# Transposing the context's fp16 halves by a DMA instead of on TensorE, in a four-stage kernel on one core

## The chip, the cores and the metric

The kernel runs on one core of one Trainium2 chip, in one launch. The metric is the device time of a run in microseconds. Three runs of the kernel before gave 470.05, 475.46 and 472.96 us, a median of 472.96 us. The profile is of one further execution, which took 474.49 us.

## The reference, cut to what matters

```python
# x: (32, 128, 256), ctx_1024: (32, 128, 256), all fp32
x = x + tanh(g_xattn[0]) * scan(layernorm(x), ctx, ctx)     # running sum of ctx * ctx with decay 0.9, times layernorm(x)
x = x + tanh(g_ffn[0])   * adapters(layernorm(x))           # x @ W.T, plus one of four low-rank adapters, picked per row
x = x + tanh(g_xattn[1]) * attention(layernorm(x), ctx, mask, Wq, Wk, Wv, Wo)
#       head_k = ctx @ Wk,  head_v = ctx @ Wv,  head_q = layernorm(x) @ Wq,  16 heads of 16,
#       sigmoid scores instead of a softmax, masked, then @ Wo
x = x + tanh(g_ffn[1])   * experts(layernorm(x))            # the best two of eight experts for each token
```

The change touches only how `ctx` gets in front of the two products `ctx @ Wk` and `ctx @ Wv`.

## The kernel before, in words

**Tiling.** The 32 batches go through in 16 pairs. One pair is 2 x 128 tokens of 256 features, and it passes stages named after their layer norms: A (the running sum), B (base and adapter product), C (queries and attention), E (router). Pairs overlap: while attention of pair p is under way, the key product of pair p + 2 is made. After the pairs, 39 tiles of 256 routed rows go through two expert layers, and the outputs are gathered and added. Each engine has its whole program written out in a fixed order (`block.sync`, `block.gpsimd`, `block.scalar`, `block.tensor`, `block.vector`); engines meet only at semaphores, and an engine that waits holds back all that stands behind it.

**Split precision.** A large product is made in three fp16 products: the high halves, and high times low both ways (`split_mm`, L1643 to L1652). So each operand exists as a high part (fp32 rounded to fp16) and a low part (fp32 minus high part, rounded).

**The context.** TensorE contracts over partitions, so it needs features on partitions, while `ctx` arrives with tokens on partitions. Before the change, for every pair p:
- SyncE loads `c_in[p % 2]` (`load_ctx`, L466).
- TensorE transposes four 128 x 128 fp32 blocks into the PSUM bank T (`transpose_ctx`, L1704, through `transposes`, L1659). The bank is shared with the transposes of B, C and E, and each waits until the one before it in the order has been copied out.
- ScalarE copies the bank to fp16 `ct_hi` (`hi_ctx`, L1075, through `hi`, L1019). VectorE subtracts and writes `ct_lo` (`lo("T", ...)`, L2456).
- TensorE makes the keys (`keys`, L1725) straight behind it, and about 10 us later the values (`values`, L1735).

ScalarE also squares `c_in` for the running sum (`squared`, L1034).

**SyncE's queue.** SyncE issues the loads, and the trip by which keys and queries are laid out by head: `keep_parts` (L476) writes a 256 KB piece to DRAM, `stack_keys` (L486, 4 DMAs) and `stack_queries` (L499, 8 DMAs) read it back to other partitions. `scores` (L1751) of a pair wait for both stacks. The queue is in order: an issue whose semaphore is not there holds all that follow.

Of the kernel before, what the change touches and what calls it, by code (L numbers as in the profile page):

```python
# [28 lines left out]
F16 = mybir.dt.float16  # L29
# [7 lines left out]
KT = D // 128  # L37
# [8 lines left out]
PROBS = 2  # L46
TOP = 2
# [36 lines left out]
def build(nc, x, ctx, mask, gates_in, temp, bp, sim, wall, wp, wu, wo, w_in, b_in, w_out, b_out, decay, eye, before,  # L84
          routing, y_rows_in, left_rows_in, out):
    st = ExitStack()
    with st:
# [140 lines left out]
        ct_hi = right("ct_hi", [128, KT, 256], F16)  # L228
        ct_lo = right("ct_lo", [128, KT, 256], F16)
# [227 lines left out]
        def _(sp):  # L457
# [158 lines left out]
            load_ctx(5)  # L616
            stack_queries(1)
# [13 lines left out]
            zero_first(7)  # L631
            stack_queries(2)
# [5 lines left out]
            stack_queries(3)  # L638
            stack_keys(4)
# [4 lines left out]
            keep_parts("q", 4)  # L644
            stack_queries(4)
# [6 lines left out]
            stack_queries(5)  # L652
            keep_parts("k", 6)
# [5 lines left out]
            stack_queries(6)  # L659
            keep_parts("k", 7)  # L660
# [6 lines left out]
            keep_parts("k", 8)  # L667
            stack_queries(7)
# [5 lines left out]
            stack_queries(8)  # L674
            keep_parts("k", 9)
# [4 lines left out]
            keep_parts("k", 10)  # L680
            stack_queries(9)
# [10 lines left out]
            stack_queries(10)  # L692
            load_ctx(14)
# [7 lines left out]
            stack_queries(11)  # L701
            keep_parts("k", 12)
# [3 lines left out]
            stack_keys(12)  # L706
            stack_queries(12)
            keep_parts("q", 13)
            stack_keys(13)
            stack_queries(13)  # L710
# [13 lines left out]
            for i in range(2, TILES):  # L724
                load_block(i)

            for n in range(NP):
                load_outputs(n)
                if PICK_BUFS - 1 <= n < ON_SP - 1 + PICK_BUFS:
                    store_pair(n + 1 - PICK_BUFS)  # L730
            for i in range(PICK_BUFS):
                sp.wait_ge(s_out[i], 16 * len(range(i, NP, PICK_BUFS)) + (16 if i == (NP - 1) % PICK_BUFS else 0))
# [3 lines left out]
        def _(pool):  # L736
# [37 lines left out]
            paused = itertools.count(2)  # L774

# [212 lines left out]
            for i in range(4, TILES):  # L988
                keep_block(i, 0)
                if i < CLOSE:  # L990
                    long_pause()
                keep_block(i, 1)

        @block.scalar
        def _(act):
# [244 lines left out]
            sigmoids(0, 1, 1)  # L1240
            sigmoids(0, 1, 0)
# [6 lines left out]
            hi_ctx(3)  # L1248
# [15 lines left out]
            normed_e(0)  # L1264
            sigmoids(1, 2, 0)
# [8 lines left out]
            hi_ctx(4)  # L1274
# [12 lines left out]
            sigmoids(2, 2, 1)  # L1287
            normed_e(1)
# [10 lines left out]
            hi_ctx(5)  # L1299
# [11 lines left out]
            normed_e(2)  # L1311
            sigmoids(3, 2, 1)
# [10 lines left out]
            hi_ctx(6)  # L1323
# [16 lines left out]
            normed_e(3)  # L1340
            gate_sigmoids(6)
# [7 lines left out]
            hi_ctx(7)  # L1349
# [14 lines left out]
            sigmoids(5, 2, 0)  # L1364
            sigmoids(5, 3, 1)
# [8 lines left out]
            hi_ctx(8)  # L1374
# [13 lines left out]
            part_hi("q", 7)  # L1388
            normed_e(5)
# [8 lines left out]
            hi_ctx(9)  # L1398
# [11 lines left out]
            sigmoids(7, 1, 0)  # L1410
            sigmoids(7, 2, 1)
# [11 lines left out]
            hi_ctx(10)  # L1423
# [11 lines left out]
            normed_e(7)  # L1435
            sigmoids(8, 2, 1)
# [10 lines left out]
            hi_ctx(11)  # L1447
# [14 lines left out]
            output_rows(7)  # L1462
            gate_sigmoids(11)
# [8 lines left out]
            hi_ctx(12)  # L1472
# [16 lines left out]
            normed_e(9)  # L1489
            sigmoids(10, 2, 0)  # L1490
# [9 lines left out]
            hi_ctx(13)  # L1500
# [10 lines left out]
            normed_e(10)  # L1511
            sigmoids(11, 2, 1)
# [8 lines left out]
            hi_ctx(14)  # L1521
# [11 lines left out]
            sigmoids(12, 1, 0)  # L1533
            sigmoids(12, 2, 1)
# [9 lines left out]
            hi_ctx(15)  # L1544
# [82 lines left out]
            for i in range(9, TILES + 1):  # L1627
                if i < TILES:
                    copy_hi(i)
                gelu(i - 1)  # L1630
                hidden_hi(i - 1)
            keep_pair(ON_SP)
            for n in range(TAIL, NP):
                copy_x3(n)
            for n in range(ON_SP + 1, NP - 1):
                keep_pair(n)
            for b in range(2):
                keep_batch(NP - 1, b)
# [3 lines left out]
        def _(pe):  # L1642
# [81 lines left out]

            def keys(last, p):  # L1725
# [9 lines left out]
            def values(last, p):  # L1735
                pe.wait_ge(s_lo["T"], p + 1)
                bank_j_free(last, "v")
                for b in range(2):
                    ins = split_mm(bank_j[:, b, :], halves(ct_hi, ct_lo, b), [wcols(k, C_V, D) for k in range(KT)])
                ins.then_inc(s_part["v"], 1)  # L1740
# [196 lines left out]
            transpose_ctx(("B", 2), 3)  # L1937
# [12 lines left out]
            transpose_c(("T", 3), 2)  # L1950
# [23 lines left out]
            transpose_ctx(("E", 0), 4)  # L1974
            project(1)
            keys(("v", 3), 4)
            transpose_c(("T", 4), 3)
# [387 lines left out]
            for i in range(7, TILES + 2):  # L2365
                if i < TILES:
                    transpose_block(i)
# [1680 lines left out]
```

## Time and profile before

| | |
|---|---|
| median of three runs | 472.96 us (470.05 to 475.46) |
| profiled execution, its time | 474.49 us |
| its span | 472.6 us |
| TensorE clock granted, mean of the span | 0.969 |
| busy: PE / DVE / ACT / POOL | 394.9 / 368.8 / 331.4 / 268.7 us |

The span is the time from the first to the last instruction that the profile shows. Busy time of an engine is the sum of its instructions' time. Matmuls are pipelined: the duration of one is longer than the distance to the next, so for TensorE the distance between starts tells what an instruction costs. "Idle before, releaser" is idle time of an engine ahead of an instruction and what ended it. Time "issue" is time in which an engine waited for nothing that the profile shows; a DMA that lands can hide in it.

### The profile page before, as it was taken

What the parts mean: (1) busy time and instruction counts of PE and PEld (TensorE: products, weight loads), DVE (VectorE), ACT (ScalarE), POOL (GpSimd) and SP (SyncE); (2) the same over time, 40 slices, a digit from 0 to 9 for tenths busy, and PEclk for the clock granted to TensorE, in tenths of its full rate; (3) what the DMA queues carried; (4) which work ended last, traced back from release to release, by engine and by line L of the source; (5) the groups of instructions that cost most, each with busy time, mean ns of one, the idle gap of its engine ahead of it and who ended that gap; (6) DMA issues with size and microseconds to landing.
All of it is one profiled execution on the core that took longest, in us unless ns stands there. A gap on an engine that the chain in (4) does not pass through costs nothing.

```text
span 472.6 us, 13099 instructions
## 1 busy us (share of the span) xinstructions
PE 394.9 (84%) x4092; PEld 308.3 (65%) x4092; DVE 368.8 (78%) x1416; ACT 331.4 (70%) x671; POOL 268.7 (57%) x313
## 2 busy tenths in 40 slices
PE   2758899998999989999899987789559999979850
PEld 1536667776776777677686765568438897967740
DVE  2888888998988889899789786367655667779994
ACT  2855788898889889898879877566706666646640
POOL 2522112545454364626545565769988888888870
PEclk9998999999999999999999999899959999999996
DMA  7245576664565555875553774624335569396985
GB/s 242 83 139 163 180 214 179 196 181 141 177 213 170 166 171 167 221 204 184 180 174 111 223 220 121 198 68 130 101 126 143 170 175 332 116 341 251 323 275 204
DMA packets 69500, 87.10 MB, mean 184 GB/s; under 512 B 9485, under 2 KB 55290, under 8 KB 69306
## 3 DMA queue, kind: packets, MB, share of 16 engines
q1 hardware_dynamic: 60074, 65.81, 46.7%
q0 software_dynamic: 6816, 18.65, 10.8%
q10 hardware_dynamic: 2544, 1.81, 1.2%
q8 instruction: 35, 0.57, 0.5%
q14 instruction: 31, 0.25, 0.2%
HBM read 51.07 MB, written 35.18 MB: 182 GB/s over the span
## 4 chain that ended last, share of the span: by engine, by line
PE 42%; POOL 17%; issue 14%; DVE 10%; DMA 8%; ACT 6%; ACTq 0%; POOLq 0%; DVEq 0%; SPq 0%
PE ps_J L1650 12%; PE ps_F L1650 6%; POOL store_y L771 6%; DMA store_y<-y_out,y_row 6%; PE ps_O L1764 5%; PE ps_T L1659 5%; POOL store_x L765 5%; PE ps_S L1751 5%; POOL pause_t L778 5%; PE ps_R L1689 2%; PE ps_O L1775 2%; PE ps_G L1650 2%; DMA temp_t<-in_temp 1%; DVE y_out L2934 1%; DVE xb_lo L2903 1%
## 5 line engine op out<-in xcount | busy, mean ns | idle before, releaser
L771 POOL DMA_INDIRECT store_y<-y_out,y_row x78 | 81.4, 1044 | 21.8 <-issue 16.5
L765 POOL DMA_INDIRECT store_x<-xn_E,slot_u x64 | 68.0, 1063 | 26.5 <-DVE slot_u L2633 13.6
L1089 ACT ACTIVATE prob<-ps_S 128x512 f32<-128x512 f32 x128 | 72.4, 594 | 12.7 <-PE ps_S L1751 10.0
L778 POOL TENSOR_TENSOR pause_t<-half_ones,minus_half 128x2 f32<-128x2 f32 x71 | 54.7, 770 | 1.9
L1751 PE MATMUL ps_S<-q_stack,k_stack 128*128 128x256 f16 x256 | 44.5, 276 | 5.9 <-issue 3.8
L2922 DVE TENSOR_TENSOR h_lo<-h_f,h_hi 128x512 f16<-128x512 f32 x39 | 26.9, 689 | 21.0 <-ACT h_hi L1173 9.4
L1650 PE MATMUL ps_J<-wout_hi,h_hi 128*128 x112 | 31.2, 278 | 14.3 <-DVE y_out L2934 10.9
L1764 PE MATMUL ps_O<-prob,v_wide 128*32 128x128 f32 x1024 | 41.0, 279 | 1.1 <-ACT prob L1089 0.5
L1165 ACT ACTIVATE h_f<-ps_F,bin_t 128x256 f32<-128x256 f32 x56 | 23.4, 470 | 24.5 <-PE ps_F L1650 18.9
L751 POOL TENSOR_TENSOR rstd_C<-var_C,minus_half 128x2 f32<-128x2 f32 x16 | 12.1, 759 | 40.4 <-DVE var_C L2412 40.4
L1650 PE MATMUL ps_F<-xb_hi,win_hi 128*128 128x256 f16 x112 | 31.7, 283 | 3.9 <-DVE xb_lo L2903 3.3
L1751 PEld LDWEIGHTS ps_S<-q_stack,k_stack 128*128 128x128 f16 x256 | 21.7, 98 | 17.3 <-issue 10.4
L1775 PE MATMUL ps_O<-wo_t,av 128*128 128x256 f32 x128 | 31.2, 387 | 1.9 <-ACT av L1117 1.5
L1764 PEld LDWEIGHTS ps_O<-prob,v_wide 128*32 128x32 f32 x1024 | 24.2, 109 | 12.3 <-issue 10.2
L1650 PE MATMUL ps_F<-xb_lo,win_hi 128*128 128x256 f16 x112 | 31.6, 283 | 0.0
L1650 PE MATMUL ps_F<-xb_hi,win_lo 128*128 128x256 f16 x112 | 31.5, 281 | 0.0
L1650 PE MATMUL ps_J<-wout_hi,h_lo 128*128 x112 | 31.1, 278 | 0.0
L1650 PE MATMUL ps_J<-wout_lo,h_hi 128*128 x112 | 31.1, 278 | 0.0
L1152 ACT ACTIVATE xb_hi<-ps_R 128x512 f16<-128x512 f32 x28 | 16.6, 594 | 19.6 <-PE ps_R L1826 15.9
L751 POOL TENSOR_TENSOR rstd_E<-var_E,minus_half 128x2 f32<-128x2 f32 x16 | 11.8, 737 | 31.0 <-DVE var_E L2412 30.8
L756 POOL TENSOR_TENSOR inv_norm<-norm2c,minus_half 128x2 f32<-128x2 f32 x16 | 11.1, 694 | 32.2 <-DVE norm2c L2481 32.2
L1775 PEld LDWEIGHTS ps_O<-wo_t,av 128*128 128x128 f32 x128 | 23.1, 190 | 6.8 <-ACT av L1117 3.5
(301 smaller groups left out, 1399.5 us busy)
## 6 DMA issues: line engine op xcount, KB each, us to landing
parts_scratch<-parts SPq DMA_DIRECT2D x32, 256.0 KB
k_stack<-parts_scratch SPq DMA_DIRECT2D x64, 128.0 KB
q_stack<-parts_scratch SPq DMA_DIRECT2D x128, 64.0 KB
xb<-store_x SPq DMA_DIRECT2D x30, 257.0 KB
y_got<-store_y SPq DMA_DIRECT2D x14, 512.0 KB
c_in<-in_ctx SPq DMA_DIRECT2D x16, 256.0 KB
x_in<-in_x SPq DMA_DIRECT2D x16, 256.0 KB
store_x<-zeros SPq DMA_DIRECT2D x15, 257.0 KB, 4.6
```

The costliest lines, as they stand in the source:

```text
L751: pool.tensor_tensor(rstd[k][q][:, :], var[k][q][:, :], minus_half[:, 0:2], ALU.pow)\
L765: pool.indirect_dma_start(store_x, bass.IndirectOffsetOnAxis(slot_u[q][:, at:at + 1], 0), xn_e[q][:, at, :], None).then_inc(s_scat[q], 16)
L771: pool.indirect_dma_start(store_y, bass.IndirectOffsetOnAxis(y_row[n][:, b:b + 1], 0), y_out[n][:, b, :], None).then_inc(s_y_kept[n], 16)
L778: pool.tensor_tensor(pause_t[:, :], half_ones[:, :], minus_half[:, 0:2], ALU.pow).then_inc(s_set_p, 1)
L1089: act.activation(prob[m % PROBS][:, 2 * n:2 * n + 2, :, :], bank_s[n], ACT.Sigmoid, scale=float(HD) ** -0.5).then_inc(s_prob[n], 1)
L1165: act.activation(h_f32[q][:, m, :], hid_banks[side(i)][:, m, :], ACT.Gelu_apprx_tanh, bias=biases[:, bass.ds(at + m, 1)]).then_inc(s_gelu, 1)
L1650: ins = pe.matmul(o, l, r, start=start and i == 0, stop=stop and i == len(seq) - 1, skip_group_check=skip)
L1659: ins = pe.transpose(bank_t[:, i, b, :], src[:, b, 128 * i:128 * i + 128], ident[:, :])
L1751: ins = pe.matmul(bank_s[n][:, g % 2, :, :], k_stack[q][:, g, k, cut], q_stack[q][:, :, g, k, cut], start=True, stop=True)
L1764: ins = pe.matmul(bank_av[32 * g:32 * g + 32, k, b, :], v_wide[q][:, b, 4 * k + g, 2 * h:2 * h + 2, :].rearrange("p a d -> p (a d)"), prob ...
L1775: ins = pe.matmul(bank_o[:, b, :], av[:, k, b, :], wo_t[:, k, :], start=(k == 0), stop=(k == KT - 1))
L2922: dve.tensor_tensor(h_lo[q][:, :, :], h_f32[q][:, :, :], h_hi[q][:, :, :], ALU.subtract) .then_inc(s_h_lo, 1)
```

## The change

For pairs 0 to 2 all is as before (`PE_CTX = 3`). From pair 3 on, the split into high and low part is made on the tokens-on-partitions layout, straight from `c_in` in SBUF into one piece `c_parts` (128 x 1024 fp16: for each of the parts, each feature half and each batch, one 128 x 128 block). One DMA, issued by SyncE, transposes the eight blocks from SBUF into `ct[p % 2]`, also in SBUF. `c_parts` and the second `ct` lie in room of the fp32 weights (`w_f32`), which is no longer needed by then. The four TensorE transposes of these pairs are gone. `keys` and `values` wait for the DMA's semaphore (`s_decay`, used again) instead of for the low part.

```diff
+PE_CTX = 3
...
-        ct_hi = right("ct_hi", [128, KT, 256], F16)
-        ct_lo = right("ct_lo", [128, KT, 256], F16)
+        ct = [right("ct", [128, 2 * KT, 256], F16),
+              w_f32[:, 0, C_K:C_Q].bitcast(F16).rearrange("p (x c) -> p x c", x=2 * KT)]
+        c_parts = w_f32[:, 1, C_K:C_Q].bitcast(F16).rearrange("p (x c) -> p x c", x=2 * KT * 2)
...
             def load_ctx(p):
-                need(sp, s_t["T"], p - 1)
+                need(sp, s_lo["T"], p - 1)
...
+            def turn_ctx(p):
+                sp.wait_ge(s_lo["T"], p + 1)
+                sp.wait_ge(s_part["k"], p - 1)
+                sp.wait_ge(s_part["v"], p - 1)
+                sp.dma_start(ct[p % 2].rearrange("p x (b s) -> p (x b) s", b=2), c_parts.rearrange("p x c -> p (x c)"),
+                             transpose=True).then_inc(s_decay, 16)
...
             def hi_ctx(p):
-                need(act, s_part["k"], p)
-                need(act, s_part["v"], p)
-                hi("T", p, ct_hi[:, :, :])
+                if p < PE_CTX:
+                    need(act, s_part["k"], p)
+                    need(act, s_part["v"], p)
+                    hi("T", p, ct[0][:, 0:KT, :])
+                    return
+                if p == PE_CTX:
+                    act.wait_ge(s_wlo, 4)
+                act.wait_ge(s_c[p % 2], 16 * (p // 2 + 1))
+                act.wait_ge(s_decay, turned(p - 1))
+                act.activation(c_parts[:, 0:2 * KT, :].rearrange("p (k b) c -> p k b c", b=2),
+                               c_in[p % 2][:, :, :].rearrange("p b (k c) -> p k b c", k=KT), ACT.Copy).then_inc(s_hi["T"], 1)
...
+            def ctx_turned(p):
+                if p < PE_CTX:
+                    pe.wait_ge(s_lo["T"], p + 1)
+                else:
+                    pe.wait_ge(s_decay, turned(p))
...
             def keys(last, p):
-                pe.wait_ge(s_lo["T"], p + 1)
+                ctx_turned(p)
                 bank_j_free(last, "k")
-                feature_major("k", C_K, ct_hi, ct_lo)
+                feature_major("k", C_K, *ctx_parts(p))
...
+            def lo_ctx(p):
+                if p < PE_CTX:
+                    lo("T", p, ct[0][:, 0:KT, :], ct[0][:, KT:2 * KT, :])
+                    return
+                dve.wait_ge(s_hi["T"], p + 1)
+                hi_part, lo_part = (c_parts[:, 2 * KT * n:2 * KT * n + 2 * KT, :].rearrange("p (k b) c -> p k b c", b=2)
+                                    for n in range(2))
+                dve.tensor_tensor(lo_part, c_in[p % 2][:, :, :].rearrange("p b (k c) -> p k b c", k=KT), hi_part,
+                                  ALU.subtract).then_inc(s_lo["T"], 1)
...
+def turned(pair):
+    return 16 * max(1, pair - PE_CTX + 2)
```

The written-out orders change so (one pair stands for all, other pairs alike). On TensorE the line `transpose_ctx` is taken out and the transpose that follows it names its new forerunner in the bank:

```diff
             add_ups(7)
-            transpose_ctx(("E", 4), 8)
             weigh(5, 3)
...
-            transpose_c(("T", 8), 7)
+            transpose_c(("E", 4), 7)
```

On ScalarE and VectorE `hi_ctx(p)` and `lo_ctx(p)` move to an earlier place, on SyncE `turn_ctx(p)` is put in:

```diff
             stack_queries(5)
+            turn_ctx(7)
             keep_parts("k", 6)
...
             keep_parts("k", 8)
+            turn_ctx(9)
             stack_queries(7)
...
             normed_e(3)
+            hi_ctx(7)
             gate_sigmoids(6)
...
             statistics_a(9)
+            lo_ctx(7)
             gain(8)
```

The places of `turn_ctx(p)` on SyncE, by the neighbours:

| pair p | stands behind | stands ahead of |
|---|---|---|
| 3 | `load_ctx(5)` | `stack_queries(1)` |
| 4 | `zero_first(7)` | `stack_queries(2)` |
| 5 | `stack_queries(3)` | `stack_keys(4)` |
| 6 | `keep_parts("q", 4)` | `stack_queries(4)` |
| 7 | `stack_queries(5)` | `keep_parts("k", 6)` |
| 8 | `stack_queries(6)` | `keep_parts("k", 7)` |
| 9 | `keep_parts("k", 8)` | `stack_queries(7)` |
| 10 | `stack_queries(8)` | `keep_parts("k", 9)` |
| 11 | `keep_parts("k", 10)` | `stack_queries(9)` |
| 12 | `stack_queries(10)` | `load_ctx(14)` |
| 13 | `stack_queries(11)` | `keep_parts("k", 12)` |
| 14 | `stack_keys(12)` | `stack_queries(12)` |
| 15 | `stack_keys(13)` | `stack_queries(13)` |

The rest of the diff writes loops of the expert stage out line by line, in the same order, and defines a helper `pause` that nothing calls.

## Rows read from the trace of the kernel before

**Rows 1.** The page: busy time (share of the span) and instructions of each engine
```profile
PE 394.9 (84%) x4092; PEld 308.3 (65%) x4092; DVE 368.8 (78%) x1416; ACT 331.4 (70%) x671; POOL 268.7 (57%) x313
```

**Rows 2.** A stretch: us, busy of PE, PEld, DVE, ACT, POOL, PEclk, DMA share, GB/s
```profile
160.00:200.00 40.00, 37.45 (x434) 29.10 (x433) 35.44 (x158) 35.12 (x74) 23.18 (x27) 1.00 0.62 178
```

**Rows 3.** The page's chain that ended last, by engine
```profile
PE 42%; POOL 17%; issue 14%; DVE 10%; DMA 8%; ACT 6%; ACTq 0%; POOLq 0%; DVEq 0%; SPq 0%
```

**Rows 4.** Instructions by tile: ns min/median/max, first and last start
```profile
L1659 PE MATMUL ps_T<-ident,c_in x64: 272/273/456, 4.2 to 262.8; 128*128 128x128 f32 x64
L1019 ACT ACTIVATE ct_hi<-ps_T x16: 574/597/607, 12.5 to 263.2; 128x512 f16<-128x512 f32 x16
L1177 ACT ACTIVATE wout_hi<-w_stage x8: 619/622/642, 19.0 to 284.5; 128x512 f16<-128x512 f32 x8
```

**Rows 5.** Timeline of PE: start, us, what, [idle before <- releaser]
```profile
159.60 0.66 PE L1659 MATMUL ps_T<-ident,c_in 128*128 128x128 f32 x4
160.09 0.27 PE L1793 MATMUL ps_F<-wu_parts,down_t 128*128 128x256 f16 x1
...
77.11 0.64 PE L1659 MATMUL ps_T<-ident,c_in 128*128 128x128 f32 x4
78.01 0.70 PE L1775 MATMUL ps_O<-wo_t,av 128*128 128x256 f32 x2 [0.26 <-ACT av L1117]
...
230.92 0.48 PE L1775 MATMUL ps_O<-wo_t,av 128*128 128x256 f32 x1 [0.29 <-ACT av L1117]
```

**Rows 6.** Waits, 40 to 300 us: us in total, times, longest
```profile
PEld ps_S L1751 <- issue: 10.2, 27, 2.2
...
PEld ps_J L1650 <- DVE ct_lo L2456: 5.3, 10, 0.8
```

**Rows 7.** Timeline: starts of the key products of pairs 5, 7, 10, 12, 13
```profile
96.16 0.10 PEld L1650 LDWEIGHTS ps_J<-ct_hi,w_hi 128*128 128x128 f16 x1 [0.35 <-DVE ct_lo L2456]
129.60 0.10 PEld L1650 LDWEIGHTS ps_J<-ct_hi,w_hi 128*128 128x128 f16 x1 [0.66 <-DVE ct_lo L2456]
180.50 0.10 PEld L1650 LDWEIGHTS ps_J<-ct_hi,w_hi 128*128 128x128 f16 x1 [0.61 <-DVE ct_lo L2456]
216.66 0.27 PE L1650 MATMUL ps_J<-ct_hi,w_hi 128*128 128x256 f16 x1
232.86 0.10 PEld L1650 LDWEIGHTS ps_J<-ct_hi,w_hi 128*128 128x128 f16 x1 [0.35 <-DVE ct_lo L2456]
```

**Rows 8.** Timeline of SyncE's queue: stack_queries of pairs 2, 3, 5, 8, 10, 11
```profile
73.97 4.94 SPq L499 DMA_DIRECT2D q_stack<-parts_scratch  x8
90.10 3.64 SPq L499 DMA_DIRECT2D q_stack<-parts_scratch  x8
125.50 3.62 SPq L499 DMA_DIRECT2D q_stack<-parts_scratch  x8
171.35 0.38 SPq L476 DMA_DIRECT2D parts_scratch<-parts  x1
173.51 5.25 SPq L499 DMA_DIRECT2D q_stack<-parts_scratch  x8
209.38 4.64 SPq L499 DMA_DIRECT2D q_stack<-parts_scratch  x8
226.79 4.45 SPq L499 DMA_DIRECT2D q_stack<-parts_scratch  x8
```

**Rows 9.** Timeline of PE: the first score products of pairs 10 and 2
```profile
215.79 0.38 PE L1751 MATMUL ps_S<-q_stack,k_stack 128*128 128x256 f16 x2 [1.06 <-issue]
81.73 0.60 PE L1751 MATMUL ps_S<-q_stack,k_stack 128*128 128x256 f16 x4
```

**Rows 10.** The page's DMA queues: packets, MB, share of 16 engines
```profile
q1 hardware_dynamic: 60074, 65.81, 46.7%
```

**Rows 11.** Timeline of ACT and DVE where hi_ctx(13) and lo_ctx(13) are put in
```profile
225.05 0.57 ACT L1089 ACTIVATE prob<-ps_S 128x512 f32<-128x512 f32 x1
224.29 0.17 DVE L2489 TENSOR_TENSOR lg<-small,inv_norm 128x8 f32<-128x8 f32 x1
```

More of the change, by code:

```diff
@@ L722, in _ @@
             stack_queries(15)
[L724 to L732, printed above, removed]
+            load_block(2)
+            load_block(3)
+            load_block(4)
@@ L986, in _ @@
             keep_block(3, 1)
[L988 to L992, printed above, removed]
+            keep_block(4, 0)
+            long_pause()
+            keep_block(4, 1)
+            keep_block(5, 0)
+            long_pause()
+            keep_block(5, 1)
+            keep_block(6, 0)
+            long_pause()
+            keep_block(6, 1)
+            keep_block(7, 0)
+            long_pause()
@@ L1625, in _ @@
             gate_ratios()
[L1627 to L1631, printed above, removed]
-            keep_pair(ON_SP)
[L1633 to L1638, printed above, removed]
+            copy_hi(9)
+            gelu(8)
+            hidden_hi(8)
@@ new lines, in _ @@
+            copy_hi(10)
+            gelu(9)
+            hidden_hi(9)
+            copy_hi(11)
+            gelu(10)
+            hidden_hi(10)
+            copy_hi(12)
+            gelu(11)
+            hidden_hi(11)
+            copy_hi(13)
+            gelu(12)
+            hidden_hi(12)
+            copy_hi(14)
+            gelu(13)
+            hidden_hi(13)
+            copy_hi(15)
+            gelu(14)
+            hidden_hi(14)
+            copy_hi(16)
+            gelu(15)
+            hidden_hi(15)
@@ L3025, in _ @@
             variances("B", 0)
-            lo("T", 0, ct_hi[:, :, :], ct_lo[:, :, :])
+            lo_ctx(0)
             scaled_similarities()
@@ L3056, in _ @@
             down_lo(0)
-            lo("T", 1, ct_hi[:, :, :], ct_lo[:, :, :])
+            lo_ctx(1)
             statistics_b(1)
@@ L3102, in _ @@
             statistics_b(2)
-            lo("T", 2, ct_hi[:, :, :], ct_lo[:, :, :])
+            lo_ctx(2)
             means("B", 2)
@@ new lines, in _ @@
+            next(gates)
+            copy_lo(21)
+            take_rows(21)
+            hidden_lo(20)
+            add_bias(19)
+            next(gates)
+            copy_lo(22)
+            take_rows(22)
+            hidden_lo(21)
+            add_bias(20)
+            next(gates)
+            copy_lo(23)
+            take_rows(23)
+            hidden_lo(22)
+            add_bias(21)
+            next(gates)
+            copy_lo(24)
+            take_rows(24)
+            hidden_lo(23)
+            add_bias(22)
@@ new lines, in _ @@
+            next(gates)
+            copy_lo(25)
+            take_rows(25)
+            hidden_lo(24)
+            add_bias(23)
+            next(gates)
+            copy_lo(26)
+            take_rows(26)
+            hidden_lo(25)
+            add_bias(24)
+            next(gates)
+            copy_lo(27)
+            take_rows(27)
+            hidden_lo(26)
+            add_bias(25)
+            next(gates)
+            copy_lo(28)
+            take_rows(28)
+            hidden_lo(27)
+            add_bias(26)
```

627 lines of the change are left out of this document (554 added, 73 removed).

## The prediction, made before the changed kernel ran

> **What bounds the kernel now.** I read the page's busy table, then the busy time by stretch, then the chain of waits, then single rows by tile and by time. Over the whole span no engine is full [rows 1], but this average mixes two stages. In the stage of pairs TensorE is busy 37.5 us of 40, VectorE 35.4, ScalarE 35.1 [rows 2]; the reader should see that TensorE is first and that two others are close behind. TensorE also leads the chain that ended last [rows 3]. The expert stage behind it is untouched, and starts as much earlier or later as the pairs end. So the question is what the change does to TensorE's in-order stream in 13 pairs. The granted clock is 1.00 there [rows 2] and I leave it so.
>
> **Removed on TensorE.** One matmul of the four is shown with 273 ns [rows 4], but they overlap: from the first transpose of pair 9 to the next instruction's start is 0.49 us [rows 5]. Where the next instruction waits for something else nothing is won: behind the transposes of pair 4 the projection waits for `av` anyway, at 78.01, and behind those of pair 13 too, at 230.92 [rows 5]. So 11 x 0.49 = 5.4 us go, against 0 for the other two.
>
> **Removed wait.** The key product waits for `ct_lo` ten times, 5.3 us in all [rows 6]. In the new order the low part is ready some 7 us ahead, so the wait goes, if the DMA is there. In pairs 5, 7, 10 and 13 it is not (below): 0.35 + 0.66 + 0.61 + 0.35 = 2.0 us stay [rows 7]. Pair 6 also waits for the bank of the product, which I count at 0.8. There remain 2.5 us. Bounds 0 and 5.3.
>
> **The split on ScalarE and VectorE.** It now reads SBUF. The nearest row is the same form on expert weights: 622 ns against 597 [rows 4]; 13 x 0.025 = 0.3 us on ScalarE, which has 4.9 us in 40 spare [rows 2], so nothing. For VectorE I take no difference. Their new order can cost: `lo_ctx(13)` is reached at 224.3, but ScalarE reaches `hi_ctx(13)` only at 225.1 and needs 0.6, so VectorE stands for 1.4 us [rows 11]; pair 7 some 0.7. VectorE has 4.6 us in 40 spare [rows 2], so I take 0.5 us; bounds 0 and 2.1.
>
> **The DMA and its place in SyncE's queue.** Nothing in the trace shows a transposing DMA. Let L be the time from when SyncE is free for it to when the data is there.
> - From below: `keep_parts` moves the same 256 KB out of SBUF; issued at 171.35 in 0.38 us, it lets the next step go at 173.51: L = 2.2 us [rows 8].
> - From above: eight blocks may cost what the eight DMAs of `stack_queries` cost, 3.6 to 5.3 us of issue [rows 8], and about 1.8 us more until used (last issue ends 214.02, scores start 215.79 behind 1.06 us of idle [rows 8, 9]): L up to 7.0 us.
> - Between: the block rows are 256 bytes, so 1024 packets. The queue's mean packet costs 0.467 x 16 x 472.6 / 60074 = 59 ns [rows 10]; 64 on each of 16 engines are 3.8 us, where `keep_parts` has 16, or 0.9. That gives L = 2.2 + 2.9 = 5.1 if a small packet costs as much as a mean one, and 2.2 if only bytes count. I take the middle, L = 3.6.
>
> The diff puts `turn_ctx` of pairs 5, 7, 8, 10, 12 and 13 behind a whole `stack_queries`. The room from the end of those issues to the key product, less 0.5 us that TensorE comes earlier, is [rows 7, 8]: pair 5, 96.16 - 93.74 - 0.5 = 1.9; pair 7, 129.60 - 129.12 - 0.5 = 0.0; pair 10, 180.50 - 178.76 - 0.5 = 1.2; pair 12, 216.66 - 214.02 - 0.5 = 2.1; pair 13, 232.86 - 231.24 - 0.5 = 1.1. The other eight have over 4 us by the same subtraction. With L = 3.6 the keys are late by 1.7 + 3.6 + 2.4 + 1.5 + 2.5 = 11.7 us. Behind `keys` on TensorE stand the next C transposes and the scores, so this goes into the path. Before scores TensorE often idles on "issue" (27 times [rows 6], 1.06 us in the one behind the late keys of pair 12 [rows 9]); such idle time absorbs a part, for which I take 0.5 us in each of the five, 2.5. Bounds 0 and 5 x 1.06. Net 9.2 us.
>
> **What is queued behind the new issue.** For pairs 3, 4, 6, 9, 11, 14 and 15 it stands ahead of `stack_queries`. Mostly it fits into the time in which SyncE waits for `keep_parts` to land. For pair 4 it does not: SyncE starts `stack_queries(2)` at 73.97 at once, ends at 78.91, and the scores start at 81.73, 1.0 us above the 1.8 that is needed [rows 8, 9]. An issue of 1.5 us costs 0.5. Bounds 0 (issue 0.38) and about 4 for all seven (issue 3.6). The waits of `turn_ctx` for key and value products of two pairs before are long met, and `load_ctx` is released by an earlier step than before: nothing.
>
> **Sum.** -5.4 - 2.5 + 0.5 + 9.2 + 0.5 = +2.3 us. On the profiled execution's own 474.49 us that is 476.8. That execution lies 1.5 us above the median of the runs, 472.96, so I forecast 475.3 us.
>
> The Trainium skill, page "Advanced Engine Details and Errata", section "X-Bar Transpose (TRN2)", says that transpose DMAs are as fast as regular ones. By that rule L would be that of `keep_parts`, and the time that of the first rival. No row here shows it.
>
> **Rival 1: the DMA is as quick as a plain one (0.20).** L = 2.2: late keys 0.3 + 2.2 + 1.0 + 0.1 + 1.1 = 4.7, of which 2.5 absorbed; sum -5.4 - 2.5 + 0.5 + 2.2 = -5.2, so 467.8 us. For it speaks that SBUF is on both sides; against it the small packets, and eight stack DMAs in flight just ahead.
>
> **Rival 2: keys wait for the DMA for long, slower (0.28).** Place: `ctx_turned` ahead of `keys`; price: 5 us for each microsecond of L above 3.6, more when the other pairs' room is used up; it decides from L = 4.1, where the sum passes +4.7. At L = 5.3 the keys are late by 20.8 us: -5.4 - 2.5 + 18.3 + 2 = +12.4, so 485.4 us. For it speaks the packet count; against it that SyncE's issue and the packets overlap.
>
> **Rival 3: the DMA is far slower, or is done block by block or element by element, so that the change does not do what it says (0.10).** At L = 7.0 all but one pair are late, 37 us in sum: -7.9 - 2.5 + 37 + 4 = +31, so 504 us and up.
>
> The Trainium skill, page "VectorE: DVE Perf Modes", section "The three transpose paths", gives 1309 ns for a 128x128 block by DMA against 390 ns on TensorE. As an estimate, eight in a row would be 10.5 us, and rival 3 would be the outcome. It speaks against this change, and no row here shows it.
>
> **Numbers.** The forecast has 0.42: L between 2.5 and 4.1, which gives 470 to 478. What a measurement can tell here is about 1%, or 4.7 us. Faster by more: rival 1 and the edge of the forecast, 0.22. Within 1%: 0.40. Slower: 0.28 + 0.10, 0.38. The range 465 to 494 us leaves out the best tail of rival 1 (0.03), the upper end of rival 2 (0.05) and rival 3 (0.10). Both signs have weight, so the likeliest case's own range is 470 to 478.
>
> **What would show it.** After the change `ps_T<-ident,c_in` has 12 instructions instead of 64. The new issue on SyncE's queue tells its own duration. Idle time of TensorE ahead of `ps_J<-ct` should be near zero in pairs 3, 4, 6, 8, 9, 11, 14, 15 and 1.5 to 3.6 us in pairs 5, 7, 10, 12, 13. If it is in all pairs, L is above 6 and rival 2 or 3 holds; if nowhere above 1 us, rival 1. VectorE should stand some 1.4 us ahead of the low part of pair 13. If scores of pairs 2, 12 and 13 start later against their stack issue, the issue itself is the price. I am wrong altogether if TensorE's stream shrinks but the pair stage does not, because VectorE, 2.1 us less busy in 40, takes over.

## The result and the profile after

The four runs of the changed kernel took 491.0, 494.0, 500.3 and 508.9 us, a median of 497.2; in the last two the granted clock was lower than in the first two, and such runs are left out of the times and ratios of this document. That leaves 492.5 us, beside 472.4 us for the kernel before (470.1 to 475.5). The ratio is 1.042, with a 95% interval of 1.030 to 1.054: slower. In a second set of runs on another chip it was 1.059 [1.050, 1.067]. On the median shown before the change the ratio gives 492.9 us. That is 17.6 us above the forecast of 475.3, and just inside the upper end of the range, 465 to 494.

I read the same views as before the change. First the page's busy line (busy time, share of the span, instructions):

```profile
PE 391.4 (80%) x4040; PEld 303.0 (62%) x4040; DVE 368.1 (75%) x1416; ACT 330.7 (68%) x671; POOL 271.0 (55%) x313
```

TensorE issues 52 instructions less, as promised, and its busy time falls by 3.5 us [rows 1]. The span grows from 472.6 to 489.2 us. So what was added is idle time. Where it was added, the first and the last start of the score products tell (count: ns min/median/max, first and last start), before and then after:

```profile
L1751 PE MATMUL ps_S<-q_stack,k_stack x256: 269/273/421, 49.3 to 306.2; 128*128 128x256 f16 x128
```

```profile
L2043 PE MATMUL ps_S<-q_stack,k_stack x256: 269/273/421, 54.2 to 322.3; 128*128 128x256 f16 x128
```

The first scores are 4.9 us late, and 11.2 us more are lost between the first and the last. The part behind them takes 166.9 us where it took 166.4: the expert stage is untouched, as predicted. Second, the instructions that touch the context's input and the new DMA (count: ns min/median/max, first and last start):

```profile
L1941 PE MATMUL ps_T<-ident,c_in x12: 272/273/445, 4.1 to 39.7; 128*128 128x128 f32 x12
L1268 ACT ACTIVATE w_f<-c_in x13: 614/622/642, 58.9 to 272.1; 128x512 f16<-128x512 f32 x13
L2903 DVE TENSOR_TENSOR w_f<-c_in,w_f x13: 657/683/693, 60.7 to 273.5; 128x512 f16<-128x512 f32 x13
L478 SPq DMA_TRANSPOSE w_f<-w_f x7: 1231/1241/1417, 61.9 to 275.4; - x7
L478 SPq DMA_TRANSPOSE ct<-w_f x6: 1231/1259/1758, 79.1 to 259.4; - x6
```

The change does what it says: 12 transposes for 64 [rows 4], 13 transposing DMAs, and each occupies SyncE's queue for about 1.25 us. The queue's packets on the page rise from 60074 [rows 10]:

```profile
q1 hardware_dynamic: 73802, 69.22, 50.6%
```

That is 13728 more, or 1056 for each DMA, close to the 1024 that I had counted. Third, the waits of TensorE and its weight loads from 40 to 300 us, those that bear on the change (total, times, longest):

```profile
PE ps_J L1932 <- DMA w_f<-w_f: 6.8, 3, 3.3
PE ps_R L1971 <- DVE moved L2880: 5.0, 1, 5.0
PEld ps_J L1932 <- DMA w_f<-w_f: 8.0, 3, 3.7
```

The wait of the key product for `ct_lo` [rows 6] is gone, and one for the DMA stands in its place. The second line is a surprise: one wait of 5 us that has nothing to do with keys. It is the longest single one, and I follow it first.

**The load of the context.** The load of pair 4's context in SyncE's queue, before and then after:

```profile
39.98 0.37 SPq L470 DMA_DIRECT2D c_in<-in_ctx  x1
```

```profile
45.08 0.37 SPq L472 DMA_DIRECT2D c_in<-in_ctx  x1
```

It goes out 5.1 us later, and `stack_queries` behind it moves by the same amount, from 43.52 to 48.68. What SyncE waits for is one row of its waits:

```profile
SPq L82 <- DVE ct L2893: 5.5, 1, 5.5
```

In the diff the buffer of `c_in` is released by VectorE's low part (`s_lo["T"]`) and no longer by TensorE's transposes (`s_t["T"]`). For pairs from 3 on that is needed; for pair 2, which TensorE still transposes, it is not, and it is later: ScalarE's and VectorE's steps come first. From there the delay goes through three in-order engines. ScalarE, VectorE and TensorE after (start, us, what, [idle before <- releaser]):

```profile
47.95 0.63 ACT L1217 ACTIVATE kv<-c_in 128x512 f32<-128x512 f32 x1 [3.36 <-DMA c_in<-in_ctx]
...
50.69 0.69 DVE L2880 TENSOR_TENSOR moved<-x,ps_R 128x512 f32<-128x512 f32 x1 [3.59 <-ACT x L1224]
...
51.52 2.04 PE L1971 MATMUL ps_R<-kv,decay_t 128*128 128x512 f32 x2 [4.97 <-DVE moved L2880]
```

Before, the last of these was

```profile
47.57 1.10 PE L1689 MATMUL ps_R<-kv,decay_t 128*128 128x512 f32 x2 [1.56 <-DVE moved L2443]
```

The same two matmuls take 2.04 us in place of 1.10. TensorE had stood idle for 4.97 us instead of 1.56, and the granted clock fell. Busy time by stretch shows it (us, PE, PEld, DVE, ACT, POOL, PEclk, DMA share, GB/s), before and then after:

```profile
48.00:56.00 8.00, 6.71 (x83) 4.90 (x82) 7.30 (x26) 5.69 (x12) 1.40 (x3) 1.00 0.64 200
```

```profile
52.00:60.00 8.00, 7.00 (x60) 4.42 (x58) 6.42 (x24) 5.42 (x13) 0.69 (x1) 0.76 0.62 191
```

So a part of that stretch ran at the lower level, 1.2 GHz. The two matmuls start 3.95 us later than before; the next of their kind, pair 5's, start 4.95 us later (70.81 for 65.86). In the second profile of the changed kernel, which spans 506.5 us, the mean over 40 to 80 us was only 0.84:

```profile
40.00:80.00 40.00, 31.98 (x268) 22.52 (x270) 27.98 (x111) 24.04 (x52) 7.25 (x10) 0.84 0.55 157
```

**The late key products.** SyncE's queue and TensorE's weight loads of pair 7 after:

```profile
133.35 3.97 SPq L508 DMA_DIRECT2D q_stack<-parts_scratch  x8
137.43 1.23 SPq L478 DMA_TRANSPOSE w_f<-w_f  x1
...
140.51 0.11 PEld L1932 LDWEIGHTS ps_J<-w_f,w_hi 128*128 128x128 f16 x2 [3.69 <-DMA w_f<-w_f]
```

From the issue to the first key product it is 3.1 us. The other late pairs answer to [rows 7]:

```profile
103.55 0.11 PEld L1932 LDWEIGHTS ps_J<-w_f,w_hi 128*128 128x128 f16 x2 [1.02 <-DMA w_f<-w_f]
192.69 0.11 PEld L1932 LDWEIGHTS ps_J<-ct,w_hi 128*128 128x128 f16 x2 [1.44 <-DMA ct<-w_f]
230.24 0.11 PEld L1932 LDWEIGHTS ps_J<-ct,w_hi 128*128 128x128 f16 x2 [0.65 <-DMA ct<-w_f]
248.24 0.11 PEld L1932 LDWEIGHTS ps_J<-w_f,w_hi 128*128 128x128 f16 x2 [3.29 <-DMA w_f<-w_f]
```

The DMAs of pairs 10 and 13 were issued

```profile
188.41 1.48 SPq L478 DMA_TRANSPOSE ct<-w_f  x1
244.65 1.23 SPq L478 DMA_TRANSPOSE w_f<-w_f  x1
```

which is 4.3 and 3.6 us ahead of their key products; in pairs 5 and 12 it is 3.2 us. These are the five pairs of the prediction: 3.69 + 1.02 + 1.44 + 0.65 + 3.29 = 10.1 us of waits. Of the other eight only pair 8 waits for its DMA, 0.25 us.

**VectorE.** One wait has grown that the prediction does not have, the step `shifts("C", p)` for GpSimd's inverse root (40 to 300 us), before and then after:

```profile
DVE shift_C L2418 <- POOL rstd_C L751: 1.6, 4, 0.8
```

```profile
DVE shift_C L2855 <- POOL rstd_C L833: 8.9, 13, 1.4
```

In the order before, the low part of the context stood in several pairs between `variances("C")` and `shifts("C")`, where it can cover GpSimd's work. The experiments ask how much of the wait that explains and whether it costs anything.

### The profile page after: what moved, and what is told of

Same layout as the page of the kernel before. It is cut to its first block, busy times and chain, and to the rows that moved or that the text cites. A ratio compares the mean times of both kernels' runs of the same rounds, so it can differ in the third digit from the quotient of the medians.

```text
span 489.2 us, 13008 instructions
## 1 busy us (share of the span) xinstructions
PE 391.4 (80%) x4040; PEld 303.0 (62%) x4040; DVE 368.1 (75%) x1416; ACT 330.7 (68%) x671; POOL 271.0 (55%) x313
## 3 DMA queue, kind: packets, MB, share of 16 engines
q0 software_dynamic: 6816, 18.65, 10.5%
## 4 chain that ended last, share of the span: by engine, by line
PE 21%; DMA 17%; POOL 17%; DVE 16%; issue 14%; SPq 8%; ACT 7%; ACTq 0%; POOLq 0%; DVEq 0%
PE ps_J L1932 8%; POOL store_x L847 6%; SPq L508 5%; DMA store_y<-y_out,y_row 5%; POOL pause_t L864 5%; POOL store_y L853 4%; PE ps_F L1932 4%; DMA parts_scratch<-parts 3%; PE ps_T L1941 2%; DMA w_f<-w_f 2%; PE ps_S L1932 2%; DMA ct<-w_f 2%; DVE y_out L3381 1%; DMA temp_t<-in_temp 1%; DMA w_stage<-in_w_out 1%
## 5 line engine op out<-in xcount | busy, mean ns | idle before, releaser
L853 POOL DMA_INDIRECT store_y<-y_out,y_row x78 | 82.5, 1057 | 20.3 <-issue 17.1
L833 POOL TENSOR_TENSOR rstd_E<-var_E,minus_half 128x2 f32<-128x2 f32 x16 | 11.8, 738 | 39.6 <-DVE var_E L2849 39.4
L838 POOL TENSOR_TENSOR inv_norm<-norm2c,minus_half 128x2 f32<-128x2 f32 x16 | 11.1, 694 | 34.7 <-DVE norm2c L2928 34.7
L1275 ACT ACTIVATE parts<-ps_J 128x512 f16<-128x512 f32 x32 | 19.0, 594 | 15.8 <-PE ps_J L1932 15.7
```

The costliest lines, as they stand in the source:

```text
L833: pool.tensor_tensor(rstd[k][q][:, :], var[k][q][:, :], minus_half[:, 0:2], ALU.pow)\
L853: pool.indirect_dma_start(store_y, bass.IndirectOffsetOnAxis(y_row[n][:, b:b + 1], 0), y_out[n][:, b, :], None).then_inc(s_y_kept[n], 16)
```

## The experiments

Three theories stood after the result. **Load**: the changed release of `c_in` costs about 5 us and the clock behind it. **Late keys**: the transposing DMA stands behind `stack_queries` in five pairs. **No gain**: even without both, the transposes that are gone don't shorten the stream, because other engines bound the pairs; its rival is that the promised 5.4 us are there and are eaten by the two faults alone. All ratios are to the kernel before on the same chip, with 95% intervals.

**1. The load released as before** where TensorE still transposes:

```diff
-                need(sp, s_lo["T"], p - 1)
+                need(sp, s_t["T"] if p - 2 < PE_CTX else s_lo["T"], p - 1)
```

> The changed kernel with one line restored in load_ctx: for pairs whose context still goes through TensorE (0 to 2), SyncE waits for their transposes again, not for their low part. Theory A (two causes: 5 us from the new wait of load_ctx(4), which holds the first stack of queries, and 11 to 12 us from key products that wait for the DMA in pairs 5, 7, 10, 12, 13): c_in(4) is issued near 40 us instead of 45.1, the first scores near 49 us instead of 54.3, and the profiled time falls by about 5 us from 491 to 486. Rival B (the DMA alone is the cause, the early delay would be regained later): the first scores come earlier, but the time stays within 2 us of 491.

Measured: 492.5 us beside 477.4, ratio 1.032 [1.026, 1.037]. The first scores start at 50.2 us, 4.0 us earlier than in the changed kernel (54.2); TensorE still waits for the DMA:

```profile
PE ps_J L1932 <- DMA w_f<-w_f: 6.7, 3, 2.6
```

So the repair takes away the load's delay and not the late keys. What it is worth this run can't say: the changed kernel was measured on other chips, and its interval of 1.042 [1.030, 1.054] overlaps this one, while that of 1.059 [1.050, 1.067] doesn't. Rival B, that the early delay is regained later, is decided by experiments 2 and 3, which ran on this chip.

**2. The transposing DMA ahead of `stack_queries`** in the five late pairs (one shown), with the load as in the change:

```diff
+            turn_ctx(7)
             stack_queries(5)
-            turn_ctx(7)
```

> The changed kernel with turn_ctx of pairs 5, 7, 10, 12, 13 moved ahead of the stack_queries behind which it stood; the load_ctx wait stays as changed. Theory A: idle of TensorE ahead of those five key products goes from 1 to 3.3 us each to under 0.5; stack_queries starts 1.3 us later each time, which the slack of the scores mostly hides; the time falls by 7 to 11 us, to 480 to 484. Rival C (the stack of queries is the tight path, and whatever is put ahead of it is paid in full): 5 x 1.3 = 6.5 us come back and the time falls by 5 us at most.

Measured: 492.6 us, ratio 1.032 [1.027, 1.037]. SyncE's queue and the key product of pair 7:

```profile
135.89 1.27 SPq L478 DMA_TRANSPOSE w_f<-w_f  x1
137.93 3.74 SPq L508 DMA_DIRECT2D q_stack<-parts_scratch  x8
...
141.54 0.17 PEld L1932 LDWEIGHTS ps_J<-w_f,w_hi 128*128 128x128 f16 x2 [0.17 <-issue]
```

No key product waits for the DMA any more. The delay of the load is still there (TensorE's wait of 5.1 us ahead of `ps_R`). The time did not fall to the 480 to 484 us that theory A had.

**3. Both repairs.**

> Both edits at once: load_ctx's wait restored for pairs 0 to 2, and turn_ctx of pairs 5, 7, 10, 12, 13 ahead of stack_queries. Theory A: the two add up, 12 to 16 us off the 491 of the changed kernel, so 475 to 479, level with the kernel before (473) or up to 1% above, since SyncE's issues of 1.25 us and the stack delays eat the 8 us that TensorE wins. If the 8 us that I costed for TensorE were real and nothing eats them, 467.

Measured: 485.0 us, ratio 1.018 [1.014, 1.023]. The two faults of the change are worth some 1.4% each when taken from the other repair alone (1.032 to 1.018, all on one chip). So the early delay is not regained later. And 1.8% stay with both mended, where I had expected at most 1%. The rival, that the promised gain is there once the faults are gone, falls here.

**4. The load's release alone**, put into the kernel before. No transpose is removed and no DMA is added:

```diff
-                need(sp, s_t["T"], p - 1)
+                need(sp, s_lo["T"], p - 1)
```

> The kernel before with one line of the change alone: load_ctx waits for the low part of the context of two pairs before, not for its transposes. No transposing DMA. Theory A: c_in(4) is issued some 5 us later, the first scores too, and the time is 477 to 479 against 473, because the pairs are a chain from there on. Rival B: the delay is early and slack takes it up, 473 to 474. In later pairs the wait may cost more, since the low part is made late there too; I expect up to 2 us.

Measured: 488.3 us, ratio 1.025 [1.020, 1.029]. The wait and its end on TensorE, where the clock again falls (2.04 us for the two matmuls):

```profile
SPq L81 <- DVE ct_lo L2456: 20.8, 5, 5.9
```

```profile
54.18 2.04 PE L1689 MATMUL ps_R<-kv,decay_t 128*128 128x512 f32 x2 [5.12 <-DVE moved L2443]
```

One word in one wait costs 2.5%, 11 us, about twice what I expected (477 to 479 against 473). But this is more than the fault of the changed kernel. Here the low part is made late in every pair, and SyncE waits for it five times from 40 us on, 20.8 us in all; in the changed kernel it waits there at pair 4's load (5.5 us) and once more for 1.7 us, because from pair 3 on the low part comes earlier. So experiment 4 shows the mechanism, and experiments 2 and 3 give its price in the changed kernel, 1.4%.

**5. No transposing DMA.** The changed kernel with the release mended and the 13 DMAs left out; keys and values of pairs 3 to 15 read the context of pair 2:

```diff
-            turn_ctx(3)
...
-                t = ct[0 if p < PE_CTX else p % 2]
+                t = ct[0]
```

> Leaves out the transposing DMAs, and so part of the computation: from pair 3 on the key and value products read what pair 2 left in ct. With the restored wait of load_ctx; the split on ScalarE and VectorE stands where the change put it. So it shows what taking 52 transposes off TensorE and reordering the split is worth if the DMA cost nothing. Theory A (the DMA's issue and its lateness eat a real gain of TensorE): 5 to 8 us below the kernel before, ratio 0.983 to 0.990. Rival D (TensorE's time was not the tight one, or the new order of the split costs as much as it wins): ratio 0.995 to 1.01.

Measured: 485.7 us beside 477.7, ratio 1.019 [1.012, 1.026]. With the DMA's issue, packets and landing all gone, the kernel is as slow as with them and both repairs. So the DMA itself is not what keeps experiment 3 above 1. Here and in experiments 10 to 12 keys and values are made from the wrong context, so the experts can get other rows; from the last scores to the end these four profiles take 166.9 to 168.7 us, the two of the kernel before 166.4 and 167.5, so that this weighs 2 us at most. The wait for the inverse root is as in the changed kernel:

```profile
DVE shift_C L2840 <- POOL rstd_C L820: 8.9, 13, 1.4
```

**6. Everything earlier**: the split right behind that of pair p - 2's C part, the transposing DMA ahead of `keep_parts("q", p - 2)`:

```diff
+            turn_ctx(7)
             keep_parts("q", 5)
...
-            turn_ctx(7)
```

> All 13 turn_ctx stand ahead of keep_parts of the queries, where SyncE idles until VectorE has made their low part, and hi_ctx and lo_ctx stand right behind the high and low part of C of the same trip, to be ready for it; with the restored wait of load_ctx. Theory A (what is left of the slowdown once the keys are on time is the 1.25 us of issue inside the trip of the queries): the time from the issue of keep_parts to that of stack_queries goes back to that of the kernel before, and the ratio to before is 0.985 to 1.00. Rival D (ScalarE and VectorE are tight there, so 0.6 + 0.7 us put ahead of the query parts are paid in each of 13 pairs): ratio 1.00 to 1.02.

Measured: 489.3 us, ratio 1.023 [1.016, 1.030]. SyncE waits for the low part of the context, ahead of the queries:

```profile
SPq L478 <- DVE w_f L2903: 8.5, 3, 4.4
```

The hoped-for 0.985 to 1.00 is not there. Whether this order is worse than that of experiment 3 can't be told: the intervals overlap (1.018 [1.014, 1.023] there), and experiment 3 has more of this wait, 11.1 us in 6 times. So earlier brought nothing, and why is not shown.

**7. The DMA alone.** The kernel before, its 64 transposes kept, with 13 transposing DMAs added at the places of experiment 3. They read `w_hi`, and nobody reads what they write:

```diff
+            def turn_ctx(p):
...
+                sp.dma_start(w_f32[:, 0, C_K:C_Q].bitcast(F16).rearrange("p (x b s) -> p (x b) s", x=2 * KT, b=2),
+                             w_hi[:, 0, 0:1024], transpose=True).then_inc(s_decay, 16)
```

> The kernel before, with its transposes on TensorE, plus 13 transposing DMAs of the same size whose result nobody reads, issued at the places of the second variant (ahead of stack_queries where they were late). Theory A: each issue lengthens the trip of the queries by about 1 us, of which a third to a half reaches the end: 4 to 8 us, ratio 1.01 to 1.017. Rival E (the transposing DMA also slows the other transfers while it runs): ratio above 1.02, and the landing times of other transfers grow. Rival F (slack hides it): ratio under 1.005.

Measured in 10 runs: 482.1 us, ratio 1.010 [1.006, 1.014]. The issues take 1.24 to 2.23 us. The wait of the scores' weight loads, which was 10.2 us before [rows 6]:

```profile
PEld ps_S L1771 <- issue: 12.6, 27, 1.8
```

Alone, on a kernel that lacks nothing else, the DMAs cost 1.0%. The wait ahead of the scores, where the stacked queries arrive, is 2.4 us longer than in the first profile of the kernel before, but in that kernel's second profile (experiment 9) it is 11.8 us, so this row does not show where the 4.7 us go. The 1.0% also does not add up with experiments 3 and 5, which differ by these DMAs and measure the same (1.018 and 1.019): I take it that the queries' steps have slack there that the kernel before doesn't have, which is argued and not shown. The prices of this kernel's delays are not a sum.

**8. The changed kernel again**, on the chip of experiments 5 to 7:

> The changed kernel once more, beside the others on one chip, so that the variants can be compared with it directly. I expect the ratio of its first measurement, 1.042, within its interval of 1.030 to 1.054.

Measured: 507.1 us, ratio 1.059 [1.050, 1.067], outside the 1.030 to 1.054 that I expected; all four runs lie at 502.0 to 508.3 us. Key products wait for the DMA five times, as in the first profile, and the longer stretch at the lower clock (0.84, shown above) sets it apart from that one. Why the clock stays low for longer here is open.

**9. The kernel before again**, one execution, profiled: 476.4 us.

> The kernel before once more, for a trace from the same chip as the next two. I expect its span 473 to 478 us, VectorE's wait for rstd_C ahead of shift_C near 1.6 us in all, and TensorE busy as in the first trace.

Its wait of `shift_C` is 1.6 us in 4 times, the same as in the first profile, so that the 8.9 us are the change's and not the chip's.

**10. No DMA, the split at its old places.** Experiment 5 with `hi_ctx` and `lo_ctx` of pairs 3 to 15 moved back:

```diff
-            lo_ctx(7)
             gain(8)
...
+            lo_ctx(7)
```

> The variant without the DMAs (it leaves out the transpose of the context from pair 3 on, key and value products read pair 2's), but with hi_ctx and lo_ctx of pairs 3 to 15 at the very places where the kernel before has them. Theory G (the steps were fillers: on VectorE the low part stood between variances C and shifts C and covered the wait for GpSimd's inverse root; moved earlier, it is paid in full and the wait too): the wait ahead of shift_C goes from 8.9 back to under 3 us and the ratio from 1.019 to 0.985 to 1.000. Rival H (the places do not matter; reading c_in instead of the bank, or the loss of TensorE's transposes as cover ahead of the projection, makes the 1.9%): ratio stays above 1.01.

Measured: 482.6 us beside 473.2, ratio 1.019 [1.014, 1.024]. The wait for the inverse root falls to 4.8 us, but SyncE's queue is held again, now by the late low part:

```profile
SPq L82 <- DVE w_f L2888: 13.8, 5, 5.0
```

The ratio is that of experiment 5, not the 0.985 to 1.000 of theory G. But the run can't tell the fillers from the load. The next one removes the load from the question.

**11. The same, the load free.** The split reads the output weights, which lie in SBUF, instead of the context:

```diff
-                need(sp, s_t["T"] if p - 2 < PE_CTX else s_lo["T"], p - 1)
+                need(sp, s_t["T"], min(p - 1, PE_CTX))
...
-                               c_in[p % 2][:, :, :].rearrange("p b (k c) -> p k b c", k=KT), ACT.Copy).then_inc(s_hi["T"], 1)
+                               wo_t[:, :, :].rearrange("p b (k c) -> p k b c", k=KT), ACT.Copy).then_inc(s_hi["T"], 1)
```

> As the variant without a transposing DMA and with the split at its old places, but the split of pairs 3 to 15 reads the output weights, which stay in SBUF, and no context; so the load of a context waits for the squared context alone and never for the late low part. It leaves out the context of pairs 3 to 15 in keys and values (they read that of pair 2). Left of the change: 52 transposes less on TensorE, the split reads SBUF. Theory 'fillers and queue': the load was what kept that variant at 1.019; the steps between variances C and shifts C stand as before, so with the queue free the ratio is 0.985 to 1.00, the wait of shift_C for rstd_C 1 to 3 us, key products 3 to 15 in 197 to 200 us. Rival 'no gain without the transposes': VectorE or ScalarE reading two SBUF inputs, or TensorE's missing cover for av, keeps it at 1.01 to 1.02, with the wait for rstd_C small all the same.

Measured in 10 runs: 476.6 us beside 471.8, ratio 1.010 [1.006, 1.013]. Here little of the change is left but the 52 transposes that TensorE no longer does. The split reads SBUF instead of the bank, and no load waits for a transpose of pairs 3 to 15; these two were not tested apart. Busy time of the long stretch of pairs, before and then here:

```profile
80.00:280.00 200.00, 186.71 (x2213) 142.39 (x2210) 175.79 (x808) 171.45 (x359) 102.87 (x121) 1.00 0.60 179
```

```profile
80.00:280.00 200.00, 182.31 (x2167) 137.93 (x2165) 175.47 (x809) 170.45 (x358) 106.07 (x122) 1.00 0.60 179
```

TensorE is busy 4.4 us less and the other engines do the same work in the same time. The stream is not shorter: pair 15's product of the running sum starts at 250.84 us, before at 250.87. TensorE is idle for what it no longer does. Its waits (40 to 300 us) show where, before and then here:

```profile
PE ps_O L1775 <- ACT av L1117: 1.5, 4, 0.6
PE ps_T L1659 <- ACT xn_C L1026: 1.1, 3, 0.6
```

```profile
PE ps_T L1928 <- ACT xn_C L1196: 5.2, 10, 1.0
PE ps_O L2052 <- ACT av L1295: 3.0, 7, 0.8
```

+4.1 and +1.5 us: the transposes of the context had stood ahead of steps that wait for ScalarE, and had covered these waits. ScalarE waits for others in turn (before and then here):

```profile
ACT xn_C L1026 <- DVE shift_C L2418: 1.5, 5, 0.6
```

```profile
DVE shift_C L2840 <- POOL rstd_C L820: 4.8, 10, 0.8
ACT xn_C L1196 <- DVE shift_C L2840: 4.3, 11, 0.9
```

So behind TensorE's wait for `xn_C` stands a chain from GpSimd's inverse root over VectorE's `shift_C` and ScalarE's `xn_C`. The wait for the root is 4.8 us with the split at its old places, where it was 1.6 before: the place of the split explains only a part of the 8.9 us.

**12. The wait for the inverse root.** Experiment 5 with `shifts("C")` of pairs 3 to 14 one step later on VectorE (one shown):

```diff
-            shifts("C", 7)
             make_x3(5)
+            shifts("C", 7)
```

> The variant without a transposing DMA, with the changed places of the split and the load released as before (1.019 in its runs, 8.9 us of waits of shift_C for rstd_C), with one edit: on VectorE shifts C of pairs 3 to 14 stands one step later, behind the step that followed it. As there, the context of pairs 3 to 15 is left out of keys and values. Theory 'cover for the inverse root': the wait for rstd_C falls to 2 to 5 us, and as the path runs from there over xn_C to the C transposes, TensorE's wait for xn_C falls too: ratio 1.008 to 1.014, where the free variant with the split at its old places had 1.010. Rival 'off the path': the wait shrinks but the ratio stays 1.016 to 1.022. Rival 'shift comes late': the steps put ahead take longer than the inverse root or wait themselves, TensorE's wait for xn_C grows, ratio above 1.022.

Measured: 485.8 us beside 477.7, ratio 1.018 [1.014, 1.022], as without it. The waits of VectorE and TensorE, first of experiment 5, then here:

```profile
PE ps_T L1928 <- ACT xn_C L1196: 2.7, 4, 1.1
```

```profile
DVE shift_C L2840 <- POOL rstd_C L820: 3.2, 6, 0.8
PE ps_T L1928 <- ACT xn_C L1196: 9.1, 11, 1.9
```

VectorE's wait falls from 8.9 to 3.2 us, and TensorE's for `xn_C` rises from 2.7 to 9.1. Covering the wait gives nothing back: `shift_C` comes later by the step put ahead of it, and the idle time turns up on TensorE. A wait on an engine names the place where the time is spent, not what it costs. What an inverse root that is ready sooner would be worth, this run does not tell.

No version measured beats the kernel before. Two more have no measurement: the whole computation with each pair's split one pair ahead, and experiment 3 with the later `shifts("C")`. So whether a better order of the split would make the change pay stays open.

## Where the prediction was right and where it was wrong

The chance for slower by more than 1% was 0.38, and the outcome is there; but the forecast said 475.3 us and the likeliest case was a kernel that stays the same. That 492.9 us still lie in the range is luck: its upper end was set for transposing DMAs slower than 3.6 us (rival 2), and what came is two terms that the sum had wrong. The prediction failed at these two steps, and one of its halves held.

**"11 x 0.49 = 5.4 us go" is the step that failed in the sum.** The removed work is real: 4.4 us less busy in 200, in experiment 11. The time did not go with it. I had checked each group of transposes against the instruction right behind it, and took two pairs out for which that one waits. But with less work ahead, the waits further on in the stream grow too: TensorE's for `xn_C` and `av` by 5.6 us in sum. A kernel with the transposes gone, no DMA and the load free measured 1.010 [1.006, 1.013], where the step promised 0.989. That the waits grew is shown; that it is the chain through GpSimd, VectorE and ScalarE which sets the pace of the pairs, and not a single busy engine, is my reading of these waits and was not tested by making one of its steps faster. That the kernel is 1.0% slower and not the same is shown by the runs and not explained: in the profiles the pairs take the same time, and the span, 474.3 us, is only 0.4% above the 472.6 of before.

**"`load_ctx` is released by an earlier step than before: nothing" was plainly wrong.** It holds neither for pair 2's buffer nor in the order of the engines: the low part follows the transposes. The statement was made from the diff and not looked up in the trace: the transposes let the load go at 39.98, the low part at 45.08. It cost 4.9 us at the first scores, with the drop of the clock (0.76 in the 8 us behind, 2.04 for 1.10 us). Its price in the changed kernel is 1.4%, some 6.5 us (experiments 2 and 3), about that of the late keys; the 2.5% [2.0, 2.9] of experiment 4 hold later loads too.

**The DMA and the late keys: right.** L = 3.6 was forecast; 3.2, 3.1, 4.3, 3.2 and 3.6 us were measured in pairs 5, 7, 10, 12 and 13, where TensorE stood waiting. The five pairs were the right ones. They wait 10.1 us in place of 11.7. Mending it is worth 1.4%, some 6.5 us, from experiment 1 to 3. "of which 2.5 absorbed" is not at odds with that, 10.1 - 2.5 being 7.6, but the intervals of the two ratios are too wide to confirm it. Rival 2, "keys wait for the DMA for long", is right in its place and wrong in its price: L passed 4.1 in one pair of the five.

The Trainium skill, page "Advanced Engine Details and Errata", section "X-Bar Transpose (TRN2)", has transposing DMAs as fast as regular ones. The trace agrees only roughly: 3.1 to 4.3 us against 2.2 us for `keep_parts` [rows 8], and 1.25 us of issue against 0.38. The other page of the Trainium skill, "VectorE: DVE Perf Modes", section "The three transpose paths", led to an estimate of 10.5 us for eight blocks; the trace does not agree, since all eight blocks take 3.1 to 4.3 us.

**"Removed wait, 2.5 us"**: the row is gone, as said. What it was worth can't be told apart, since it sits in the same stream as the transposes.

**"For VectorE I take no difference", order 0.5 us**: its instruction is the same, 683 ns. The stand ahead of pair 13's low part, forecast as 1.4 us, is 0.26 us in the trace of the changed kernel. The order may have cost more than 0.5 in another way. Between experiments 5 and 11 (the split at the change's places, 1.019, and at its old ones with a free load, 1.010) lie 0.9%, some 4 us, which would be above the bound of 2.1; but the intervals still overlap between 1.012 and 1.013, and the two differ in the load and the split's source too, so this size is not certain. Where within the order it would be spent stays open; covering the wait for the inverse root did not give it back (experiment 12).

**"An issue of 1.5 us costs 0.5", bounds 0 and 4**: the issue is 1.25 us. Thirteen of them alone cost 1.0% [0.6, 1.4], 4.7 us, at the places of experiment 3, which can't be told from the bound, and nothing that can be measured between experiments 3 and 5.

In sum the changed kernel is 20 us slower (492.9 for 472.96) where +2.3 was forecast. With 0 in place of -5.4, and 6.5 in place of nothing for the load, the sum would be +14.2. The 6 us that are left the runs do not place with certainty: the order of the split is one candidate, and the 1.0% of experiment 11 another.

What I said would show me wrong altogether was that "TensorE's stream shrinks but the pair stage does not". That is what came in experiment 11, though not as I had it: VectorE's busy time did not take over, the waits grew.

## What to carry to other kernels

When work is taken off the busiest engine of a pipeline and two others are close behind it (here 35.4 and 35.1 us of 40 beside 37.5), take the gain as zero until the waits behind each removed piece are shown to be short; the piece may be what covers them. Look up every changed wait of a queue in the trace, above all a release that seems harmless: what the new releaser is, when it ends, and what is queued behind the waiting instruction. And a new transfer in a shared in-order queue should go out before a long batch of issues: standing behind it cost 1.4% here. Putting it still earlier brought nothing that could be measured.

## What the runs showed of the hardware

- An idle gap of about 5 us on TensorE in an otherwise busy stage was followed by a granted clock of 0.76 over the next 8 us, with matmuls at twice their time (two of 128x512 in 2.04 us for 1.10); after the gap of 1.56 us at the same place the clock stayed at 1.00. The distance to the kernel before grew by 1.0 us from there to pair 5 (3.95 to 4.95 us), so the delay grew while the clock was low. The drop came again in experiment 4 and in the second profile of the changed kernel.
- One transposing DMA from SBUF to SBUF, 128 x 1024 fp16, held SyncE's queue for 1.23 to 1.76 us in the first profile, where a plain 256 KB one takes 0.38. In the second profile of the changed kernel one took 2.49 us, in experiment 7 one took 2.23. In the five pairs that waited for it, the key product started 3.1 to 4.3 us after the issue began. Each made 1056 packets.
